# An attention layer with a hand-written order of work: shift stages on other steps, zeros for the operand rows, a narrower wait and another engine for LayerNorm 2 in the last body

## What is computed

```python
qkv = layer_norm(x, g1, be1) @ w_qkv
q, k, v = (qkv[:, 0], qkv[:, 1], qkv[:, 2])
scores = jnp.einsum('nhd,mhd->hnm', q, k) * SCALE
mask = (adj != 0)[None, :, :]
scores = jnp.where(mask, scores, -jnp.inf)
attn = jax.nn.softmax(scores, axis=-1)
out = jnp.einsum('hnm,mhd->nhd', attn, v).reshape(n, DIM)
x = x + out @ w_proj + b_proj
h2 = layer_norm(x, g2, be2)
ff = jax.nn.gelu(h2 @ w1 + b1) @ w2 + b2
return x + ff
```

## Time and profile before

| what | value |
|---|---|
| median of 3 runs | 1753.01 us (1752.37 to 1755.19) |
| the profiled execution | 1753.59 us, span of its instructions 1751.4 us |
| PE, DVE, ACT, POOL busy | 92%, 81%, 74%, 67% of the span |
| mean granted TensorE clock | 0.975 of full speed |
| DMA | 119.67 MB in 174086 packets |

### The profile page before, as it was taken

The page is one execution under the profiler, slowest core; times in us unless marked ns, Lnnn a source line. Parts: engine busy times, 40 slices in busy tenths (PEclk is TensorE's granted clock), DMA queues, the critical chain, the costliest instruction groups (busy, mean ns, idle before and its releaser), DMA issues.

```text
span 1751.4 us, 46484 instructions
## 1 busy us (share of the span) xinstructions
PE 1607.2 (92%) x17016; PEld 506.6 (29%) x17016; DVE 1415.1 (81%) x4474; ACT 1295.0 (74%) x1425; POOL 1173.4 (67%) x1108
## 2 busy tenths in 40 slices
PE   6989999999999999999999999999999999999975
PEld 3422222323223232323223232323223232323213
DVE  6888889887998888887998889887998789987501
ACT  4547777787777877787777877778787877777871
POOL 4944587469856687459856688558865698557441
PEclk9869999999999999999999999999999999999995
DMA  8710046202550045301460035401461035300000
GB/s 213 181 43 2 13 131 119 59 2 69 141 116 2 1 135 117 74 2 57 131 127 13 2 119 127 80 2 37 144 113 34 2 104 133 65 1 2 7 7 6
DMA packets 174086, 119.67 MB, mean 68 GB/s; under 512 B 140193, under 2 KB 154402, under 8 KB 173858
## 3 DMA queue, kind: packets, MB, share of 16 engines
q1 hardware_dynamic: 163106, 108.30, 25.8%
q10 hardware_dynamic: 10752, 8.39, 1.7%
HBM read 77.08 MB, written 6.03 MB: 47 GB/s over the span
## 4 chain that ended last, share of the span: by engine, by line
PE 58%; ACT 20%; issue 13%; POOL 5%; DVE 2%; DMA 1%; SPq 0%; ACTq 0%; POOLq 0%; DVEq 0%
ACT probs L763 17%; PE pv_ps L1063 15%; PE ring_ps L999 11%; PE score_ps L1153 10%; PE score_ps L1168 10%; POOL probs L545 2%; PE ring_ps L1119 2%; ACT q_stack L649 2%; PE score_ps L1085 2%; PE score_ps L1024 2%; PE ring_ps L1110 1%; PE ring_ps L1095 1%; PE ring_ps L1102 1%; DVE masked_out L798 1%; DMA adj_in<-adj 1%
## 5 line engine op out<-in xcount | busy, mean ns | idle before, releaser
L798 DVE CUSTOM_DVE_ANT_0 masked_out<-ring_ps,row_mask 128x512 bf16<-128x512 f32 x2048 | 1311.0, 688 | 166.4 <-PE ring_ps L999 127.4
L763 ACT ACTIVATE probs<-score_ps,score_scale 128x1024 f32<-128x1024 f32 x1024 | 1087.9, 1111 | 349.0 <-PE score_ps L1168 341.1
L545 POOL TENSOR_TENSOR probs<-probs,keep 128x1024 int32<-128x1024 int32 x256 | 604.6, 2362 | 292.1 <-ACT probs L763 281.1
L1063 PE MATMUL pv_ps<-probs,v_ones 128*17 128x512 f32 x4096 | 539.4, 599 | 6.6 <-POOL probs L545 5.6
L999 PE MATMUL ring_ps<-k_stack,q_stack 51*64 51x512 f16 x4096 | 489.8, 397 | 14.1 <-DVE row_max L798 13.3
L1168 PE MATMUL score_ps<-q_stack,k_stack 51*64 51x512 f16 x4096 | 372.1, 391 | 33.2 <-ACT probs L763 13.9
L1153 PE MATMUL score_ps<-mask_t,ident_bf 64*64 64x512 bf16 x3072 | 276.6, 387 | 49.3 <-ACT probs L763 18.6
L999 PEld LDWEIGHTS ring_ps<-k_stack,q_stack 51*64 51x64 f16 x4096 | 166.4, 104 | 464.4 <-DVE row_max L798 411.0
L1168 PEld LDWEIGHTS score_ps<-q_stack,k_stack 51*64 51x64 f16 x4096 | 116.7, 104 | 242.8 <-PE score_ps L1153 185.1
L798 DVE DVE_READ_ACCUMULATOR2_ANT row_max<- 128x1 f32 x2048 | 169.8, 83 | 0.0
L1153 PEld LDWEIGHTS score_ps<-mask_t,ident_bf 64*64 64x64 bf16 x3072 | 94.0, 105 | 193.4 <-ACT probs L763 132.5
(11 more groups left out here) (116 smaller groups left out, 808.2 us busy)
## 6 DMA issues: line engine op xcount, KB each, us to landing
adj_in<-adj SPq DMA_DIRECT2D x128, 512.0 KB, 4.1
q_stack<-q_dram SPq DMA_DIRECT2D x42, 64.0 KB, 3.4
mask_t<-row_mask SPq DMA_TRANSPOSE x128, 3.5
xq<-xnT_dram ACTq DMA_DIRECT2D x8, 256.0 KB, 2.7
x_res<-x ACTq DMA_DIRECT2D x8, 256.0 KB, 4.4
out<-rows ACTq DMA_DIRECT2D x8, 256.0 KB, 2.6
xnT_dram<-attn ACTq DMA_DIRECT2D x4, 256.0 KB, 4.8
xnT_dram<-halves ACTq DMA_DIRECT2D x4, 256.0 KB, 2.4
```

The source lines that it names most:

```text
L545: nc.gpsimd.tensor_tensor(view, view, keep[:, KEPT.index(m), :].unsqueeze(1).broadcast_to([128, 2, TILE]), ALU.mult).then_inc(probs_masked, 1)
L763: nc.scalar.activation(probs[:, (2 * g + n) % SLOTS, :], score_ps[:, half:half + 2, :].rearrange("p a n -> p (a n)"), ACT.Exp, scale=score ...
L798: nc.vector.tensor_tensor_reduce(out=masked_out[:, place % 3, :], in0=ring_ps[:, place % 3, :], in1=row_mask[:, j, ch * 512:(ch + 1) * 512 ...
L1063: last = nc.tensor.matmul(pv_ps[32 * k:32 * k + HD + 1, :], v_ones[:, block_of(g, b), 2 * p + a, :], probs[:, (2 * g + b) % SLOTS, a * TIL ...
```

## The change

The edits are these. The shift stages move to other steps, all odd, and the second pair's two stages change their order. Two loads of zeros into the shift rows of `q_stack` are added to each load of the queries, from a small buffer stored once at the start. A new function `free` gives the count that an item waits for: in bodies with attention the old one, in the last body that of the last item in the same bank. The first up matmul waits for the copy of h2t explicitly. POOL's wait in `split_max` follows the new steps. In the last body DVE makes the Newton steps and the application of LayerNorm 2 (`end_norm2`), and POOL only adds the bias.

```diff
-ACT_FILLS = {17: ("h2t",), 33: ("q",)}
+H2T_STEP = 17
+ACT_FILLS = {H2T_STEP: ("h2t",), 33: ("q",)}
 ACT_FILLS.update({g: ("up", f) for f, g in enumerate(UP_STEPS)})
-for _p in range(1, PAIRS + 1):
-    ACT_FILLS.update({QUARTER * _p - 12: ("shift", _p % PAIRS, 0), QUARTER * _p - 2: ("shift", _p % PAIRS, 1)})
+
+SHIFT_STEP = {(1, 0): 5, (1, 1): 13, (2, 1): 29, (2, 0): 31, (3, 0): 37, (3, 1): 45, (0, 0): 53, (0, 1): 61}
+ACT_FILLS.update({g: ("shift",) + w for w, g in SHIFT_STEP.items()})
...
+Q_LOADS = 2 * (len(PART_ROW) + 1)
...
+        zero_dram = nc.dram_tensor("zero_dram", (SHIFT_PARTS + 1, PAIRS, TILE), F16, kind="Internal").ap()
...
+        def free(ring, i, bcd, place, turn):
+
+            held = [p for p in ring.held(*bcd) if p <= place - turn and (place - p) % turn == 0]
+            if bcd[1]:
+                return made(ring, i, bcd, place - turn)
+            return made(ring, i, bcd, held[-1]) if held else ring.before(i)
...
+            sp.wait_ge(q_clear, 2)
+            settled(sp)
+            sp.dma_start(zero_dram, q_stack[1][SHIFT_ROW:SHIFT_ROW + SHIFT_PARTS + 1, :, :]).then_inc(zero_stored, 16)
...
-                    sp.wait_ge(q_in, i * (16 * 2 * len(PART_ROW)))
+                    sp.wait_ge(q_in, i * (16 * Q_LOADS))
...
                 sp.wait_ge(q_stored, (i + 1) * 32)
+                sp.wait_ge(zero_stored, 16)
                 settled(sp)
...
+                for a in range(2):
+                    r = HALF * a + SHIFT_ROW
+                    sp.dma_start(q_stack[1 - par][r:r + SHIFT_PARTS + 1, :, :], zero_dram).then_inc(q_in, 16)
...
-                    at = QUARTER * (p - 1 if p else PAIRS - 1) - (12, 2)[jj]
-                    pool.wait_ge(score_full, made(SCORES, i, bcd, ACT_PLACE[at]) if at > 0 else
-                                 SCORES.before(i) + SCORES.upto(bcd, ACT_PLACE[at + STEPS] - SCORE_PLACES))
+                    at = ACT_PLACE[SHIFT_STEP[(p - 1) % PAIRS, jj]]
+                    pool.wait_ge(score_full, made(SCORES, i, bcd, at) if p != 1 else
+                                 SCORES.before(i) + SCORES.upto(bcd, at - SCORE_PLACES))
...
-                    if d and g in POOL_LN2:
+                    if d and g in POOL_LN2 and (c or g == POOL_LN2[-1]):
                         layer_norm2(i, POOL_LN2.index(g))
...
+            def end_norm2(i):
+
+                first = (i - 1) * ROOT_OPS
+                dve.wait_ge(ln2_step, (i - 1) * LN2_STEPS + LN2_STATS)
+                for k in range(NEWTON):
+                    if k > 0:
+                        dve.wait_ge(root_step, first + 4 * k)
+                    nc.vector.tensor_tensor(newton[:, :], rstd[:, :], rstd[:, :], ALU.mult).then_inc(root_step, 1)
+                    dve.wait_ge(root_step, first + 4 * k + 1)
+                    nc.vector.tensor_tensor(newton[:, :], newton[:, :], inv_var[:, :], ALU.mult).then_inc(root_step, 1)
+                    dve.wait_ge(root_step, first + 4 * k + 2)
+                    nc.vector.tensor_scalar(newton[:, :], newton[:, :], -0.5, 1.5, ALU.mult, ALU.add).then_inc(root_step, 1)
+                    dve.wait_ge(root_step, first + 4 * k + 3)
+                    nc.vector.tensor_tensor(rstd[:, :], rstd[:, :], newton[:, :], ALU.mult).then_inc(root_step, 1)
+                dve.wait_ge(root_step, first + ROOT_OPS)
+                for s in range(SUB):
+                    nc.vector.tensor_scalar(rows2[:, s, :], x_res[:, s, :], mean_var[:, s, 0:1], rstd[:, s:s + 1],
+                                            ALU.subtract, ALU.mult).then_inc(ln2_applied, 1)
...
                         if x == 1 and d and LN2_STEP <= g < LN2_STEP + 4:
                             layer_norm2(i, bcd, g - LN2_STEP)
+                            if not c and g == LN2_STEP + 3:
+                                end_norm2(i)
...
-                    pe.wait_ge(score_taken, made(SCORES, i, bcd, place - 2))
+                    pe.wait_ge(score_taken, free(SCORES, i, bcd, place, 2))
...
                     f = what[1]
+                    if f == 0:
+                        pe.wait_ge(score_taken, made(SCORES, i, bcd, ACT_PLACE[H2T_STEP]))
...
-                pe.wait_ge(row_taken, made(ROWS, i, bcd, place - 3))
+                pe.wait_ge(row_taken, free(ROWS, i, bcd, place, 3))
...
-                        pe.wait_ge(q_in, (i + 1) * (16 * 2 * len(PART_ROW)))
+                        pe.wait_ge(q_in, (i + 1) * (16 * Q_LOADS))
```

More of the change, by code:

```diff
@@ L325, in program @@
         xq_loaded, q_done, q_clear = sem("xq_loaded"), sem("q_done"), sem("q_clear")
-        q_stored, q_in = sem("q_stored"), sem("q_in")
+        q_stored, q_in, zero_stored = sem("q_stored"), sem("q_in"), sem("zero_stored")
         row_full, row_taken, score_full, score_taken = (sem("row_full"), sem("row_taken"), sem("score_full"),
```

## The result

The changed kernel takes 1721.66 us (median of 4 runs, 1720.98 to 1722.52), the kernel before 1754.1 beside it on the same chip (4 runs, 1752.37 to 1755.97). The ratio is 0.9816, its 95% interval 0.9805 to 0.9828: 32 us faster, where 30.7 were forecast and 1722.3 was the predicted time. The profiled execution took 1722.52 us with a span of 1720.7, 30.7 less than the span before; the mean granted clock went from 0.975 to 0.982.

A forecast was written before the change was run, and what follows sets the result against it. PE was taken to bound the kernel, through its waits and needless work. Moved stages 17.5, tail waits 4.9, LayerNorm 2 4.4 and clock 3.9 sum to 30.7 us, from 1753.0 to 1722.3; range 1713 to 1733.

The forecast's parts named there:

- LayerNorm 2: In the tail, moving the root and application from POOL to DVE cuts 8.07 us to 3.6, saving 4.4.
- Even stages: Shift stages on even steps of the bodies cost 0.75 us at most steps, 0.72 at step 20; 32.6 us together.
- Odd stages: The same shift stages on odd steps cost 0.28 us each, 15.1 us over 54; moving them saves 17.5 us.
- signs that were to show it: In the bodies: pairs with a moved shift near 5.74 us instead of 6.21, no PE wait on the shift's copy.
- The "up" row: In the bodies, an FFN up matmul on an odd step costs 1.16 us, PE's own 1.13 and 0.03.
- Steps 28 to 31: Stage at 29 costs 0, since PE waits for POOL at step 30 anyway; pair 30 and 31 stays unchanged.
- Rival (c): In the bodies, moved stages cost what they cost now, so only the tail gains: 1739.8 us; chance 0.12.
- rival (d): On odd steps the next masks wait for ACT's whole copy, 1.02 us a stage: 1770.4 us; chance 0.04.
- The tail's waits: PE's waits for the previous item's reader in back, projections, ups and downs all go, saving 4.9 us.
- The tail's clock: With ups and downs nearly gap-free, the clock rises 6.2 us into the ups, a net saving of 3.9 us.
- Rival (a): In the tail, the clock does not rise before the end: 1727.4 us; chance 0.13.
- Rival (b): In the tail, the clock opens far sooner, already in the projections, giving 10 us for 3.9: 1716.2 us; chance 0.10.

The follow-up runs named there:

- three copies: Changed kernel with a third ACT copy of the same size, to a spare tile, ahead of the two of each shift stage: 1728.52 us, ratio 0.9864.
- LayerNorm 2 alone: Kernel before with only LayerNorm 2's root and application moved to DVE in the last body, old waits kept: 1748.84 us, ratio 0.9970.
- narrow wait only: Kernel before with only `free` and the first up's explicit wait in the last body, LayerNorm 2 left on POOL: 1739.97 us, ratio 0.9926.
- last stage behind: Changed kernel with two stages back at steps 4 and 36, scores reordered between masks, and step 31's stage behind the values' matmul: 1714.04 us, ratio 0.9764.

## Why the prediction was right and wrong, point by point

**Even stages.** Taken at 0.75, they cost 0.77; step 20 taken at 0.72, it was 0.85. Over 30 and 8 stages that is 0.6 and 1.0 us more saved than forecast.

**Odd stages: the term that was mis-sized.** "The shift's 0.22 becomes 0.22 to 0.32 ... I take 0.28" was wrong; a stage costs 0.40. The step that failed is "ACT's copy ends about when the masks want the bank". The copies start only when ACT's group of four exponentials is done and take 0.74 together. At steps 13, 45, 53 and 61, 30 stages, the masks come 0.2 to 0.3 us too early, and the kernels with one and with three copies show that this is the missing part. At steps 5 and 37, 16 stages, it is not: there the copies' number changes next to nothing, the pairs grew by 0.19 each where 0.06 was forecast (pairs 4 and 6 together for step 5), and what PE waits for is the exponential ahead of the transposes, 0.16. The forecast had this exponential end "just as PE gets there" and put 0.06 on it and the copy together. The 46 stages together cost 46 x (0.40 - 0.28) = 5.5 us, with the 0.22 that steps 4 and 36 were taken to cost before, which no run measured. The upper bound, 0.38 a stage, was also too low. Two of the signs that were to show it came out on the wrong side: the pairs took 5.86 and not 5.74, and PE's weight loads did wait for the copy. The "up" row that I argued from pays PE's time alone; the masks behind it (L1153, at 1185.88 in the trace of before) run in one piece, although its two readers on ACT (L725 and L726, 0.69 and 0.68 us) end only at 1186.03. Its matmuls take PE 1.12 us where a stage's transposes take 0.22; whether that makes the difference, no run tests.

**Steps 28 to 31.** The stage at 29 was to be free and the one at 31 to cost 0.28, less the 0.1 of the old step 30. Measured, pair 28 got 0.41 longer and pair 30 0.45 shorter: the two together are 12.96 against 13.00. The stage at 29 is paid at once and comes back from POOL's wait at step 30. That it nets to nothing was right; step 31 turned out free as well, 1.8 us in my favour. The forecast that pair 30 would be unchanged was wrong.

**The sum for the bodies** then comes near: 17.5 + 0.6 + 1.0 - 5.5 + 1.8 = 15.4 against 14.7 measured (the lengths of bodies 0 and 7 are not in these medians; the two kernels without the zeros saved 15.8 and 15.9, 1.0 more in body 0, by the clock). Rival (c), that the stages go on costing what they cost, and rival (d), that they cost 1.02 each, are both out; (d) had the right mechanism, the wait for the copies, and a fraction of the size, 0.2 where it priced 0.74.

**The zeros.** Forecast 0, measured 0.0. The two loads took 0.61 us of the SP queue, less than the 0.9 taken. What the operand rows hold changed no length that can be seen: the row units' matmuls, which read them, took a mean of 397 ns with the zeros and 397 without.

**LayerNorm 2.** Forecast 8.07 to 3.6, saved 4.4; measured 3.67 and 4.4. The pitch of DVE's small operations is 0.20, and the four applications take 1.12 with POOL idle, as the 1.11 of the earlier trace rows. The 2.77 of the earlier trace rows came with POOL at work for 2.30 of them. The case in which both engines are at work beside each other did not occur in this stretch (POOL's bias starts at 1705.53, behind the applications), and no run shows what made those 2.77 longer.

**The tail's waits.** Forecast 4.9. The idle time in ups and downs went as listed, 3.4 us, and the first part of the tail got 2.2 us shorter where 1.5 was counted, since the back and projection matmuls, now each in one run, also take 0.6 less time: together 5.6.

**The tail's clock.** I let it rise 6.2 us into the ups and took 3.9. It rose 3.0 us into them, and gave 5.3 + 4.3 - 3.4 = 6.2 us. The step that failed is the borrowed 6.2, which was how long the downs of the kernel before had run at the low level (0.50 from 1740.0 to 1746.2, then 1.00; the last two groups of downs took 1.70 and 1.16 us where the first two took 2.04 and 2.08, which is the 1.24 of the forecast); over all kernels with packed ups the rise came 3.0 to 5.5 us into them, and 3.0, the changed kernel's, is the earliest of these. Rival (a) is out. Rival (b) was half right: the ups' clock did open sooner, but the projections stayed low. In the other nine kernels with packed matmuls it rose while the projections still ran, as (b) had it, but fell again ahead of the ups in all of them. The runs with one part each show that here the narrower wait makes the difference: with it alone the clock rose 3.5 us into the ups, with LayerNorm 2 alone it stayed at 0.50 through them. What sets the moment of the rise, no run shows.

**The total was closer than its terms.** The bodies came out 2.8 us under the forecast and the tail 2.9 over it. The two errors cancel, so 1722.3 against 1721.66 says less for the reasoning than it seems to.

## What to carry to other kernels

Put a small item that another engine must read back on the step after which its bank is wanted last, then find when the reader really comes free: here the copies could not start before a group of four exponentials ended, and where the masks came too early each further 0.36 us of copy cost 0.2 to 0.3. Work inserted between the item and the next user of its bank (here the scores of the other block) is another way than making the item smaller (it took 3.2 us off the bodies; leaving out one of the two copies took 7.1). In this tail, with few matmuls, the waits of 0.4 to 0.8 us between them cost 5.6 us in all, and then 6.2 again in clock.

## What the runs showed of the hardware that was not expected

**A rise of the clock can fall into a pause.** After the change, the packed "back" and projection matmuls ran at 0.50 from 1694.0 to 1700.3, the clock was at 1.00 for 3.4 us in which PE did nothing, and it was low again when the transposes came (windows of the tail, above). With the narrow wait only, the rise came at 1710.5 with projections left to do, and they took 2.66 us instead of 3.78. That is 1.1 us between kernels with the same order of matmuls in this place. Over the ten kernels with packed matmuls the projections took 2.61 to 3.78 us and the ups 5.35 to 6.39; the changed kernel has the longest of the one and the shortest of the other.

**Low stretches in the set-up go with a later start.** The first exponential came at 121.1 us before, 121.4 after, 118.7 with three copies and 117.9 with the last stage behind, though the set-up was hardly changed. The windows of the first 100 us have a clock of 0.91 before and 0.98 in the last of these:

```profile
0.00:100.00 100.00, 80.75 (x378) 37.27 (x378) 76.78 (x246) 55.64 (x95) 73.39 (x97) 0.91 0.77 188
```

```profile
0.00:100.00 100.00, 77.77 (x390) 35.11 (x390) 81.25 (x256) 57.30 (x97) 75.42 (x101) 0.98 0.74 189
```

Over the fourteen profiles the first exponential came at 117.9 us with 3.4 us of the first 100 at 0.50, at 118.7 with 10.2, at 119.3 to 120.3 with 13.7, and at 120.9 to 121.5 with 17 to 20.5. Such differences of up to 3.6 us are as large as what most of the later experiments are about. The share of low clock does vary between executions of one kernel: among the runs of the kernel before, one of 1750.65 us had a mean of 0.979 and one of 1756.05 a mean of 0.974. Whether a kernel also has its own share in it cannot be told from one profile of each.

**Matmuls that stand out of the program's order.** The four transposes of a stage appear in the timeline at 1244.95 and 1245.00 with the first two of the values' matmuls between them (timeline of PE, above), although the program has all four ahead. Whether PE ran them so or the records' starts only make it look so, no run here tells. On the even step, behind the values' matmuls, they stood together for 0.29 us.
